# Listing the tiles of attention's first two groups first, and starting the mix with first halves of sequences inside the last expert slots

## The reference

```python
x = x + attn_a(layernorm(x))   # linear attention along a sequence, q,k = elu+1, projected by W_o
x = x + ffn(layernorm(x))      # top-1 of 8 experts: gate * (relu(x W1 + b1) W2 + b2), d_ff 512
x = x + attn_b(layernorm(x))   # prev[t] = x[t-1] + d * prev[t-1]; gate sigmoid(r) * (v Wv Wo)
x = x + ffn(layernorm(x))
```

## Time and profile before

| | before |
|---|---|
| median of 3 runs (range) | 287.8 us (287.49 to 288.69) |
| the profiled execution: its time, its span | 288.31 us, 286.6 us |
| PE busy (share of span), instructions | 270.5 us (94%), 2343 |
| DVE busy (share of span), instructions | 227.2 us (79%), 1030 |
| ACT busy | 183.8 us (64%), 564 |
| POOL busy | 219.0 us (76%), 304 |
| the chain that ended last, by engine | PE 63%, DVE 18%, DMA 5%, SP's queue 4%, POOL 3% |
| HBM read, written | 14.60 MB, 11.57 MB |

### The profile page before, as it was taken

How to read it: one execution, slowest core, us unless ns; L and a number is a source line. 1 busy time by engine, 2 the same in 40 slices (tenths; PEclk the granted TensorE clock), 3 DMA queues, 4 the chain that set the end, 5 groups by cost and what they waited for, 6 DMA issues and landing times.

```text
span 286.6 us, 8102 instructions
## 1 busy us (share of the span) xinstructions
PE 270.5 (94%) x2343; PEld 239.6 (84%) x2343; DVE 227.2 (79%) x1030; ACT 183.8 (64%) x564; POOL 219.0 (76%) x304
## 2 busy tenths in 40 slices
PE   7989999987899999999999799999899999999994
PEld 7766666654598999999994488898699999999994
DVE  4797999997786987788771589999947988777873
ACT  2686666531599788888870276563289976676661
POOL 3956288777868898886553888888778888888875
PEclk9999999998999999999999999999899999999999
DMA  5799950011413655331103800101324244332210
GB/s 133 212 260 321 172 88 31 28 41 53 120 39 86 131 109 114 100 80 47 39 18 75 225 1 0 49 29 40 90 64 115 76 119 101 108 94 71 66 42 4
DMA packets 32652, 25.73 MB, mean 90 GB/s; under 512 B 6129, under 2 KB 28914, under 8 KB 32609
## 3 DMA queue, kind: packets, MB, share of 16 engines
q1 hardware_dynamic: 27456, 16.54, 25.5%
q0 software_dynamic: 4576, 8.57, 9.0%
q10 hardware_dynamic: 576, 0.10, 0.2%
HBM read 14.60 MB, written 11.57 MB: 91 GB/s over the span
## 4 chain that ended last, share of the span: by engine, by line
PE 63%; DVE 18%; DMA 5%; SPq 4%; issue 3%; POOL 3%; ACT 2%; DVEq 0%; ACTq 0%; POOLq 0%
PE pair L1911 21%; PE pair L1897 15%; PE bank L1897 7%; PE bank L1887 3%; SPq L374 3%; PE pair L1831 2%; DVE rows L996 2%; PE bank L1780 2%; DVE stats L1011 2%; PE pair L1763 2%; PE pair L1824 2%; PE pair L1661 2%; DMA rows<-x_mid 2%; DVE am L1118 1%; DVE sc L1220 1%
## 5 line engine op out<-in xcount | busy, mean ns | idle before, releaser
L1911 PE MATMUL pair<-w2s,hT 128*128 x624 | 82.7, 276 | 0.1
L532 POOL DMA_INDIRECT sorted<-rows,place x64 | 66.5, 1039 | 18.2 <-issue 14.9
L1911 PEld LDWEIGHTS pair<-w2s,hT 128*128 128x128 f32 x624 | 75.7, 192 | 0.4 <-issue 0.2
L1897 PE MATMUL pair<-xsT,w1s 128*128 128x128 f32 x406 | 57.7, 278 | 0.9 <-ACT xsT L796 0.9
L1897 PEld LDWEIGHTS pair<-xsT,w1s 128*128 128x128 f32 x406 | 51.5, 194 | 1.9 <-DVE tm L1229 1.0
L719 ACT COPY w1s<-w1all 128x516 f32 x78 | 49.7, 638 | 0.6 <-issue 0.4
L555 POOL DMA_INDIRECT x_mid<-ys,xs x39 | 38.5, 986 | 13.9 <-DVE ys L1421 9.4
L555 POOL DMA_INDIRECT out<-ys,xs x39 | 38.6, 989 | 9.1 <-issue 7.2
L796 ACT COPY xsT<-bank 128x128 f32<-128x128 f32 x78 | 20.8, 267 | 37.2 <-PE bank L1887 36.3
L1411 DVE SCALAR_TENSOR_TENSOR ys<-pair,xs 128x128 f32<-128x128 f32 x78 | 27.0, 347 | 21.3 <-PE pair L1911 20.9
L801 ACT ACTIVATE hT<-pair,w1s 128x128 f32<-128x128 f32 x117 | 34.8, 375 | 1.1 <-PE pair L1897 1.1
(11 more groups left out here) (184 smaller groups left out, 499.3 us busy)
## 6 DMA issues: line engine op xcount, KB each, us to landing
xs<-sorted SPq DMA_DIRECT2D x78, 66.0 KB, 2.3
rows<-x_mid SPq DMA_DIRECT2D x8, 260.0 KB, 5.1
w1all<-in_L_ffn_W_b SPq DMA_DIRECT2D x8, 258.0 KB, 6.0
rows<-in_L_attn_a_x SPq DMA_DIRECT2D x16, 128.0 KB, 2.7
w2s<-in_L_ffn_W SPq DMA_DIRECT2D x8, 256.0 KB, 5.3
sorted<-pad SPq DMA_DIRECT2D x30, 66.0 KB
sorted<-rows,place POOLq DMA_INDIRECT x64, 2.6
x_mid<-ys,xs POOLq DMA_INDIRECT x39, 2.6
```

The lines of the kernel that those rows point to most:

```text
L532: pool.indirect_dma_start(sorted_rows[l], bass.IndirectOffsetOnAxis(ap=place[:, t:t + 1], axis=0), rows[:, t, :], None).then_inc(s_sent[l] ...
L1897: mm = nc.tensor.matmul(bank[2 + 2 * half + i % 2][:, c * P:(c + 1) * P], w1s[i % NW][:, f:f + P], xsT[i % NB][:], start=True, stop=True)
L1911: mm = nc.tensor.matmul(bank[6 + i % 2][:, 0:P], hT[i % NB][:, c], w2s[:, bass.ds(e, 1), c, :].rearrange("p o d -> p (o d)"), start=(c == ...
```

## The change

The tables of layer zero's stages 1 and 2 are made by new steps (`wide_step`) that list the tiles which hold rows of attention's first two groups (`OPENING` = 2) ahead of the others, by which all of those are done by slot 28 (`OPENED_BY` = 29). A table's step works on 16 columns per slot (8 experts, early and late) where it worked on 8, and there are more steps. The choice of the last group moves from slots 3 and 4 to slots 5 and 6; COUNT_AT stays 7. The mix's groups are taken in another order: first halves of two sequences, then their second halves. The first two groups are loaded in the last slots of layer zero, and their scales (POOL) and norms (ACT, DVE) and the transposes of the first (PE) are put between those slots' own instructions. The products that nobody reads are left out at the boundary.

```diff
+OPENING = 2
+    OPENED_BY = sum(n for _, n in STAGES[0][:-1]) + E
 # SP
-                src = x_src[l].rearrange("(n p) d -> p n d", p=P)
-                sp.dma_start(rows[:, tiles(g), 0:XM], src[:, tiles(g), :]).then_inc(s_x_in[g], 16)
+                pair, c, s = g // 4, g // 2 % 2, g % 2
+                src = x_src[l].rearrange("(r s c j p) d -> p r s c j d", s=2, c=2, j=GT, p=P)
+                sp.dma_start(rows[:, tiles(g), 0:XM], src[:, pair, s, c]).then_inc(s_x_in[g], 16)
...
+                if l == 0:
+                    for i in range(OPENED_BY - ND, OPENED_BY):
+                        sp.wait_ge(s_sct[i % ND], dmas(0, i, ND))
+                    load_x(1, 0)
+                    load_x(1, 1)
                 for i in range(ST - ND, ST):
                     sp.wait_ge(s_sct[i % ND], ring_total(l + 1, i % ND, ND))
 # POOL, experts(0)
                     scatter(l, i)
+                    if l == 0 and i == ST - 6:
+                        new_row_numbers()
+                    if l == 0 and i == ST - 5:
+                        scales(BS, 0)
+                    if l == 0 and i == ST - 3:
+                        scales(BS, 1)
...
-            for b in range(len(MIX_NORM_BATCHES) - 1):
+            for b in range(2, len(MIX_NORM_BATCHES) - 2):
                 scales(BS, b)
...
-                if k == 1:
-                    scales(BS, len(MIX_NORM_BATCHES) - 1)
+                if k in (1, 2):
+                    scales(BS, len(MIX_NORM_BATCHES) - 3 + k)
 # ACT
+            def norm_opening(j):
+                act.wait_ge(BS["rs1"], 2)
+                act.wait_ge(AS["xT"], NG)
+                nc.scalar.activation(xn[0][:, j], val(j), ACT.Identity, bias=nmr1[:, j:j + 1],
+                                     scale=rstd1[:, j:j + 1]).then_inc(BS["xn"], 1)
...
-                    if i == CHOOSE_AT + 2:
+                    if i == CHOOSE_AT + (4, 2)[l]:
                         lexp(l, (AS, BS)[l], LASTB)
                     if i + 3 < ST:
                         copy_w1(l, i + 3)
+                    if l == 0 and i == ST - 4:
+                        norm_opening(0)
+                    if l == 0 and i == ST - 3:
+                        norm_opening(1)
 # DVE
-                after(dve, BS["scan"], g)
-                if p == 1:
-                    nc.vector.tensor_copy(sc[1][:, 0:1], sc[0][:, GW:GW + 1])
+                after(dve, BS["scan"], g - 1)
+                goes_on = g % 4 >= 2
+                if goes_on:
+                    nc.vector.tensor_copy(sc[p][:, 0:1], sc[p][:, GW:GW + 1])
+                else:
+                    nc.vector.memset(sc[p][:, 0:1], 0.0)
...
+            def wide_step(s, step):
...
+                if step == "low":
+                    nc.vector.tensor_tensor(low[:, w], ranks[:, w, FULL], need[:, 1], ALU.min
...
+                if step == "past":
+                    nc.vector.tensor_tensor(pastw[:, i], slot_i[0][:, i].unsqueeze(2).to_broadcast([1, count, 2 * E]),
+                                            per_slot(cumw[:, w]), ALU.is_ge)
...
+                if step == "weigh":
+                    nc.vector.tensor_tensor(weighw[:, i], pastw[:, i], per_slot(step_on[:]), ALU.mult
...
-                        if i == CHOOSE_AT + 1:
+                        if i == CHOOSE_AT + 3:
                             one_hot(0, AS, LASTB)
...
+                        if i in (ST - 3, ST - 2):
+                            norm_opening(GT // 2 + i - (ST - 3))
...
+                        if i == ST - 1:
+                            evac_half_of_first()
+                            norm_half_of_mix(1)
                         add_y(i)
 # PE
+                    if l == 0 and i == ST - 1:
+                        transpose_x(BS, 0)
                     second(i)
...
-            keep_clock(8)
-            pe.wait_ge(s_x_in[0], 48)
-            keep_clock(1)
-            transpose_x(BS, 0)
             for k in range(NG + 1):
                 mix_slot(k)
```

More of the change, by code:

```diff
@@ L100, in hybrid_block @@
         assert sum(slots for _, slots in stages) == ST and stages[-1][0] == LASTB
+    WIDEST = [s for s in range(1, len(STAGES[0]))]
+    GONE, MID, FULL = slice(0, E), slice(E, 2 * E), slice(2 * E + 1, 3 * E + 1)
+    early = OPENING * GW // P + E - 1
+    assert early - STAGES[0][-2][1] <= E
+    OPENED_BY = sum(n for _, n in STAGES[0][:-1]) + E
     CAP = TOK + P
@@ L772, in mix_slot @@
                     return
+                if k == 0:
+                    evac_xT(BS, 1, "mix")
+                    gates_of_mix(0)
+                    return
+                if k == 1:
+                    norm(BS, 2)
+                    evac_x2T(0)
+                    evac_xT(BS, 2, "mix")
+                    row_veps(BS, 0)
+                    return
+                if k == 2:
+                    norm(BS, 3)
                 if k + 1 < NG:
@@ L1335, in table_step, with needed_step @@
                                             ).then_inc(s_gone[l], 1)
+            def needed_step(step):
+                if step == "tiles":
+                    dve.wait_ge(s_table[0], 8)
+                    so_far = posb[OPENING - 1][0:1, GT * len(ROUTE_BATCHES[OPENING - 1])]
+                    nc.vector.scalar_tensor_tensor(out=need[:, 0], in0=so_far, scalar=1.0 / P, in1=whole8[:, 1],
+                                                   op0=ALU.mult, op1=ALU.add).then_inc(s_table[0], 1)
+                if step == "round":
+                    dve.wait_ge(s_table[0], 9)
+                    nc.vector.tensor_scalar(need[:, 1], need[:, 0], ROUND, -ROUND, ALU.add, ALU.add
+                                            ).then_inc(s_table[0], 1)
@@ L1855, in mix_slot @@
             def mix_slot(k):
-                if k == 0:
+                if k <= 2:
                     mix_rows(k)
-                if k + 1 < NG:
+                if k + 1 < NG and k != 1:
                     transpose_x(BS, k + 1)
```

241 lines of the change are left out of this document (177 added, 64 removed).

## The result

The changed kernel takes 292.73 us, a median of 4 runs from 291.04 to 294.22, beside 287.64 for the kernel before in the same comparison. The ratio is 1.0172 with a 95% interval of 1.012 to 1.0225. The forecast was 287.9 in a range of 283.2 to 290.4: the change is slower, and the range does not hold it. The profiled execution took 293.58 us, with a span of 291.9, and so stands 0.85 above the median. Medians are of all executions, while the ratios leave out as slow those more than 1.5% above the fastest of their kernel.

A forecast was written before the change was run, and what follows sets the result against it. PE was taken as the bound, full in layer zero's later slots, with some 8 us empty at the boundary. Terms -3.97 + 0.3 + 1.46 + 1.70 + 0 + 0.6 = +0.09 on 288.31: median 287.9 us, range 283.2 to 290.4.

The forecast's parts named there:

- The choice of the last group: Slot 7: the choice, behind the norm of slot 9's tile, makes PE's count start later, +1.46 us.
- The clock: Behind slot 7's new wait: the granted clock falls to 0.50 for 3.40 us, +1.70 us, with 0 as lower end.
- The wider tables: Slots 1 to 4 and 10 to 12: longer DVE rows cost PE 0 us, bounds 0 and 1.5.
- The boundary: Layer zero to mix: last scatter 3.7 us later, group 2's transposes 1.59 earlier, its scan products 3.97 us earlier.
- its clock: Boundary: two PE idle times of 2.2 and 2.7 us can let the clock fall, +0.6 us, between 0 and 1.7.
- The batches 4 and 5: Mix's slots: a batch of eight tiles that came before the sends now stands between them, +0.3 us (0 to 0.7).
- 149.41: Layer zero's last slots: the time at which the prediction had scales(0) end.
- 164.35: Boundary: the time at which the prediction had PE's transposes of group 2 start, where they started at 165.94.
- the slower ones: Rivals: DVE falling behind (290.2, chance 0.18), POOL held up by DVE (289.4, 0.05), no early opening (near 291, 0.03).
- DVE falling behind: Rival, slots 1 to 4 and 10 to 12: small rows make DVE late, +2.4 us, 290.2; chance 0.18.
- POOL held up by DVE: Rival, the three scales that gate PE: DVE's work slows POOL, 1.2 to 2.4 us more, about 289.4; chance 0.05.
- the three signs by which the prediction would know itself wrong: No PE wait at slot 7; last scatter not later; mix's middle waiting for scans rather than group 2's load.

The follow-up runs named there:

- e2: The changed kernel with the choice of the last group in DVE's slots 4 and 5 in place of 5 and 6: 290.7 us, ratio 1.0118.
- e4: The kernel before with only the choice of the last group moved, to DVE's slots 5 and 6 from 3 and 4: 292.51 us, ratio 1.0157.
- e3: The changed kernel with four products that nobody reads on PE ahead of the count in slot 7: 293.5 us, ratio 1.0199.
- e8: The changed kernel with two products that nobody reads on PE ahead of the count in slot 7: 291.38 us, ratio 1.0141.
- e6: The changed kernel with e1's and e2's edits, and scales of groups 0 and 1 behind the scatters of slots 32 and 38: 287.8 us, ratio 0.9997.
- e7: e6 with stage 2's table spread over two more slots of DVE (10 to 13 for its wide rows): 287.78 us, ratio 1.0002.
- e1: The changed kernel with the scales of the mix's last batch (groups 6 and 7) in mix slot 1, not 2: 291.28 us, ratio 1.0102.
- e10: e7 with groups 0 and 1 scaled as one batch behind slot 32's scatter, and six unread products ahead of group 2's transposes: 283.28 us, ratio 0.9815.
- e11: The changed kernel with six products that nobody reads on PE ahead of group 2's transposes: 294.72 us, ratio 1.0222.

## Why the prediction was wrong, step by step

- **The choice of the last group, +1.46:** right. The count is 1.54 late, and e2 and e4 show that the place of the choice alone makes it.
- **The clock, +1.70:** right in size, 1.5 us. That the wait lets it fall is borne out by all fourteen profiles (five with wait and fall, nine with neither), among them e3 and e8, in which `oh` is as late but PE is not idle.
- **The wider tables, 0 with bounds 0 and 1.5:** wrong step, "with PE at half speed in those very slots, DVE catches up". The clock was back at 96.7 us, and the rows of 288 elements ran from 101.8. They cost 1.05 us in e2, and 0.74 of what they cost go when they are spread (e6 to e7).
- **The boundary, -3.97, and its clock, +0.6:** the mechanism was right, the waits came where they were named (2.12, 2.42 and 1.93 us against some 2.2). But the clock fell in the last slots themselves, where it is on the path of the last scatter: that came 4.23 later and not 3.7, group 2's transposes gained 0.67 and not 1.59, and the whole was -2.99 where -3.4 had been summed. Two times in its working, 149.41 and 164.35, stand 0.1 above what the named rows give (149.33 and 164.25), which moves no term by more than 0.1.
- **The batches 4 and 5, +0.3 (0 to 0.7):** the step that failed and decided the outcome; it measured 4.70. From group 3's products of rows to layer one the changed kernel took 3.68 us more, and 1.02 more before that, where PE waits for norms that used to be done early (0.70 at 177.65 for group 4's). The prediction named the sends between which the batch now stands, but not the path that leads on from there: the batch and three sends hold up POOL's row scales of group 2, these DVE's choice, and that PE's count (1.99 us of wait), and the clock falls behind the wait (3.53 us for products that take 1.97). e1 shows that moving one batch back takes 3.14 us of that stretch away, the wait and the slow products behind it. That POOL was also held up by DVE in just that batch, for some 1.35 us, is part of the wait of 1.99; in e1 POOL has such rows too (rstd 2.18, nmean 1.12), and no wait follows.
- **The chances.** Up to group 2's scan products the terms summed to -0.2, and +1.10 was measured. The case that came true, a wait for POOL in the middle of the mix and a further fall of the clock behind it, was not among the rivals; the slower ones ended at 291. Of those, DVE falling behind came true by its half in slots 10 to 12. POOL held up by DVE did not come in the scales that gate PE, where the rival had it (2.07 us for group 0, 2.04 for group 1, 2.13 for group 2). It came later in the mix: in nmr (1.19 us at 182.36, beside a scan of DVE, and 0.20 at 175.71 without one), in rstd of the same batch (2.03 against 1.67), and in the row scales of group 0 (1.97 at 170.86, beside a scan, and 1.04 at 178.37). The Trainium skill (SBUF — State Buffer, "Who interferes with whom") says that a DVE instruction with two inputs in SBUF contends with a GpSimd instruction that reads SBUF; the nmr rows agree with it. That is narrower than the prediction's "whenever DVE has work beside the scales". Of the three signs by which the prediction would know itself wrong none showed: PE waited at slot 7, the last scatter was later, and the mix's middle did not wait for scans.

The sum with measured terms: 1.54 + 1.5 + 1.0 - 2.99 + 1.02 + 3.68 - 1.08 = 4.7 of 5.3 us. Of the rest 0.5 lies in layer one's slots 5 to 38 (63.31 against 62.78 us); the same stretch takes 62.8 to 63.8 in other profiles with the same code there, and I have no cause for it.

## What to carry to other kernels

Where work is put ahead of time into a full pipeline, price the queue that it is put on, and price it by who waits behind it: here the scales took 2.1 us a batch, and what cost was the scatters, evacuations and row scales behind them. When something is moved out of a quiet place into a busy one (a batch of scales from ahead of the sends to between them), follow it to the engine that bounds the time, two or three releases on. And when a wait of PE can't be removed, try products that nobody reads in it. In the profiles of e8 and e10, where they end before or with the wait, the clock stayed up behind them; in e3 they outlasted the wait and held up the count, and in e11 an earlier wait had already let the clock fall.

## What was not expected of the hardware

The spread between executions of this program goes mostly with the clock. In 51 executions of the kernel before, the mean granted clock was from 0.986 to 1.0; five more, at 291.6 to 292.4 us, had 0.982. In the 20 at 0.988 or below the time was 288.2 to 289.5 us; in the 25 at 0.994 or above it was 285.4 to 287.8, but for three at 288.1 to 289.8. The same waits let the clock fall in one execution and not in another: the wait of 1.88 us ahead of 68.45 was followed by 3.40 us at 0.50 in the profile of before, and in e2's profile, where PE waits the same 1.88 us at 68.0, the clock stays at 1.00 there. So a stretch at half clock that one profile shows can be missing in the next execution, and a term like the 1.70 of the prediction belongs in a range.
